# Values of all heads computed ahead, node-major, tile by tile, in a one-core graph transformer layer

## The chip, the cores and the metric

One core of a Trainium2 chip runs the whole program in one launch. The metric is device time in microseconds (us) of that core, the median of three runs. TensorE is called PE below, VectorE DVE, ScalarE ACT, GpSimd POOL, and SyncE, which only issues DMAs here, SP.

## What is computed

1250 nodes with 1024 features, 40,000 edges, all in float32. The layer adds to `x` a graph convolution branch and a linear attention branch of the normalized input, and then a mixture of experts of the normalized sum:

```python
xn = _layernorm(x, axis=-1)
x = x + gnn(xn, src, dst, ...) + mix(xn, Wq, Wk, Wv, proj, Wo, bo)
x = x + ffn(_layernorm(x), Wr, W1, W2)
...
# mix: 16 heads of 64 columns, 256 random features
q, k, v = heads(xn @ Wq), heads(xn @ Wk), heads(xn @ Wv)
q_prime, k_prime = relu(q @ proj), relu(k @ proj)
kv = einsum('bhsf,bhsd->bhfd', k_prime, v)
attn = einsum('bhsf,bhfd->bhsd', q_prime, kv) / (q_prime . sum(k_prime) + EPS)
mix = attn @ Wo + bo
```

The change is in the attention branch (in how `v` is made) and in the opening of the kernel, where `x` is normalized.

## The kernel before

Every float32 operand of a product is split into a high and a low part of type fp32r, and each product is three matmuls (`COMBOS`: high by high, high by low, low by high). ACT makes the high part, DVE the low part as the difference.

The nodes are cut into ten tiles of 125 (`NT`, `T`). In the opening all ten `x` tiles are loaded into one buffer `dx`; DVE takes the statistics of each (step `LN`, L1158), ACT normalizes it in place (`LNB`, L835), SP stores it to `xn_d`, PE transposes it in eight 128-column blocks (`XT`, L1667), and ACT and DVE split it into `big_hi` and `big_lo`, which hold the normalized input feature-major for all nodes.

After that the 16 heads are done in 8 pairs. A pair needs three slabs, `V`, `K`, `Q`, each 128 columns of a weight matrix: the slab is loaded two ahead, split (step `P`), and multiplied over all nodes in `slab_product` (L1553; 8 contraction blocks `kt` x 3 combinations x 3 chunks of 418 columns). The value slab comes out feature-major, is copied to `vT` and transposed again in ten blocks (`VT`, L1657) into `v_hi`, `v_lo`, node-major. Then ten `KK` steps (L1678) make the key features of each tile, ten `KV` steps (L1692) sum keys by values, `S` turns the result, `QP` (L1715) makes the query features of each head and `AT` (L1724) the attention of each head; `RC` divides (one 8 us reciprocal on DVE), `RH` splits the result.

Besides, the adjacency matrix is built in DRAM (`adj_d`) by 80 groups of 500 edges: DVE writes one-hot tables (`EO`, eight operations of L1050 for each group), PE multiplies them (`group_product`, L1500), ACT copies the sum to one of three `stage` buffers (`E`), POOL adds it to `adj_d` by an accumulating DMA (L734), one after the other. Group products lie inside slab products, after the block numbers that `PARTS` names. The identity matrix (`eye`) is written to `adj_d` before the first add.

All engines walk the same hand-written list `ORDER` (function `steps`, L89) and do their part of each step in that order; `with_split(key)` puts the split of the next slab, the one-hots and stage copies of the groups inside, and the slab itself. PE writes into two large PSUM slots in turn (`places_of`), and waits in `free_slot` until the slot's former content has been read. `find_bases` (L1061) and `find_keys` (L1071) make the group bases and keys from the edge lists; the one-hots need them. SP walks `ORDER` too, and waits in place for what a DMA needs.

Of the kernel before, what the change touches and what calls it, by code (L numbers as in the profile page):

```python
# [69 lines left out]
def groups_within():  # L70

    share = {("V", 0): 2, ("K", 0): 4, ("Q", 0): 4}
    for p in range(1, PAIRS):
        share[("K", p)], share[("V", p)] = 6, 4
    within, g = {}, 0
    for key in SLABS:
# [8 lines left out]
LN_TILES = ((0, 2), (2, 5), (5, 8), (8, 10))  # L85
PARTS = {0: (), 2: (5, 7), 4: (3, 4, 6, 7), 6: (2, 3, 5, 6)}


def steps():  # L89
# [10 lines left out]
    o = ln(0, 1) + [("LNS", 0), ("BASE",), ("LNB", 0), ("LNB", 1)] + ln(2, 3, 4) + [("LNS", 1), ("LNB", 2)]  # L100
    o += ln(5, 6) + [("XT", 0), ("LNB", 3), ("XT", 1)] + ln(7) + [("LNS", 2), ("LNB", 4), ("XT", 2), ("LNB", 5)]
    o += ln(8) + [("XT", 3), ("LNB", 6)] + ln(9) + [("LNS", 3), ("LNB", 7), ("XT", 4), ("LNB", 8), ("XT", 5)]
    o += [("LNB", 9), ("XT", 6), ("XT", 7), ("WR",), ("P", 0), ("XT", 8), ("XT", 9), ("MP",), ("BASE2",)]
    o += with_split(("V", 0)) + with_split(("K", 0), [("XC",)]) + [("VT", 0)] + with_split(("Q", 0))
    for p in range(PAIRS):
# [67 lines left out]
ORDER = steps()  # L173
AMID = {6: ("RT", 0), 7: ("PX", 0), 9: ("RT", 1)}
PSUM_KINDS = {"DG", "DT", "Z", "H", "HT", "XT", "V", "VT", "K", "Q", "KK", "QP", "AT",
              "O", "OT", "N", "FT", "R", "RT", "PX"}
ACT_KINDS = PSUM_KINDS - {"OT", "PX", "DG", "DT", "Q", "N"} | {"P", "ZP", "KC", "S", "RH", "LNB", "MP", "RP", "QE"}
DVE_KINDS = {"ZP", "Z", "P", "XT", "VT", "K", "QE", "KK", "S", "QP", "RC", "RH", "OT", "N", "DG", "DT",
# [13 lines left out]
def places_of():  # L192

    place, before, last, turn = {}, {}, {}, 0
    for k in ORDER:
# [4 lines left out]
        elif k[0] == "OT":  # L200
# [54 lines left out]
def build(nc, x, src_cols, dst_cols, dst_groups, slabs, w1, w2, wr, proj, feat_rows, consts, turns, tie,  # L255
          iota, keys, eye, pe, blank, before, list_blank, tokens, expert_at, b2_rows, out):
    ctx = ExitStack()
    with ctx:
# [38 lines left out]
        wr_raw = at("wr_raw", BIG + 8192 + 12288, [128, KD * EXP])  # L297

        dx = at("dx", R + 45600, [T, NT, D])
# [46 lines left out]
        vt = at("vT", R + 20096, [128, NP])  # L346

        v_p = [at(f"v_{'hl'[q]}", R + 25120 + 7680 * q, [T, NT, 192], F32R) for q in range(2)]
        qp_p = [at(f"qp_{'hl'[q]}", R + 45600 + 10048 * q, [128, 2, NP], F32R) for q in range(2)]
# [9 lines left out]
        proj_raw = at("proj_raw", R + 93056, [128, 2 * FEAT])  # L359
# [57 lines left out]
        xn_d = nc.dram_tensor("xn_d", [N, D], F32, kind="Internal").ap()  # L417
        h_d = nc.dram_tensor("h_d", [KD, T, NT * 128], F32, kind="Internal").ap()
# [46 lines left out]
        xn_stored = sem("xn_stored")  # L465
# [73 lines left out]
        def v_psum(ps):  # L539
            return ps[:T, :NT * 128].rearrange("p (j h c) -> p j h c", h=2, c=64)  # L540
# [5 lines left out]
        def _(sp):  # L546
# [5 lines left out]
            for i in range(2):  # L552
                spread(dx[:, i, :], x[T * i:T * i + T, :], x_landed[i])
            sp.dma_start(grp_i[:, :], dst_groups).then_inc(edges_in, 16)
            sp.dma_start(ident[:, :], consts).then_inc(ident_in, 16)
            for i in range(2, 5):
                spread(dx[:, i, :], x[T * i:T * i + T, :], x_landed[i])
            for i in range(5, NT):
                spread(dx[:, i, :], x[T * i:T * i + T, :], x_landed[i])
            sp.dma_start(slab_raw[0][:, :], slabs[0]).then_inc(slab_landed[0], 16)  # L560
# [6 lines left out]
            sp.dma_start(slab_raw[1][:, :], slabs[1]).then_inc(slab_landed[1], 16)  # L567
# [36 lines left out]
            for k in ORDER:  # L604
                if k[0] == "LNB":
                    i = k[1]
                    sp.wait_ge(act_done, ACTED[k])
                    spread(xn_d[T * i:T * i + T, :], dx[:, i, :], xn_stored)
# [9 lines left out]
                elif k == ("RP", 2):  # L618
                    sp.wait_ge(act_done, ACTED[k])
                    sp.wait_ge(dve_done, DVED[k])  # L620
                    sp.wait_ge(xn_stored, LAND * NT)
# [93 lines left out]
        def _(pool):  # L715
# [6 lines left out]
            for q in range(2):  # L722
                pool.memset(v_p[q][:, :, 64:128].bitcast(F32), 1.0 - q).then_inc(memset_done, 1)
                pool.memset(big[q][:, :, N:NP].bitcast(F32), 0.0).then_inc(memset_done, 1)
            pool.wait_ge(slab_landed[0], 16)
# [3 lines left out]
            for g in range(NG):  # L729
                first = pool.value_load(base_i[0:1, g:g + 1], min_val=0, max_val=N - 1)  # L730
# [71 lines left out]
        def _(act):  # L802
# [13 lines left out]
            for k in ORDER:  # L816
# [11 lines left out]
                if kind == "LNS":  # L828
                    a, b = LN_TILES[k[1]]
                    if k[1] == 0:  # L830
                        act.wait_ge(memset_done, 7)
# [1078 lines left out]
```

## Time and profile before

| | |
|---|---|
| median of 3 runs | 1594.02 us (1593.66 to 1599.02) |
| time of the profiled execution | 1595.89 us |
| its span, first to last instruction | 1594.0 us |
| PE busy | 1474.5 us, 93% |
| DVE busy | 819.7 us, 51% |
| ACT busy | 510.2 us, 32% |
| mean granted clock of TensorE | 0.974 |
| chain that ended last | PE 78%, DVE 9%, ACT 6%, DMA 3%, issue 3% |

The page of a profile gives the busy time of each engine, the span in 40 slices, the chain of waits and the costliest groups of instructions. The timeline gives instructions in order of time, merged where several of one kind follow each other; in brackets is the idle time of the engine ahead of an instruction, and what ended it. A windows row gives, for a stretch of time, the busy time of each engine, the granted TensorE clock (1.00 is 2.4 GHz, 0.50 is 1.2 GHz), the share of the DMA engines and the GB/s that they moved. Ends of PE instructions are modelled and overlap with the next; the distance from start to start is the honest measure there.

### The profile page before, as it was taken

What the parts mean: (1) busy time and instruction counts of PE and PEld (TensorE: products, weight loads), DVE (VectorE), ACT (ScalarE), POOL (GpSimd) and SP (SyncE); (2) the same over time, 40 slices, a digit from 0 to 9 for tenths busy, and PEclk for the clock granted to TensorE, in tenths of its full rate; (3) what the DMA queues carried; (4) which work ended last, traced back from release to release, by engine and by line L of the source; (5) the groups of instructions that cost most, each with busy time, mean ns of one, the idle gap of its engine ahead of it and who ended that gap; (6) DMA issues with size and microseconds to landing.
All of it is one profiled execution on the core that took longest, in us unless ns stands there. A gap on an engine that the chain in (4) does not pass through costs nothing.

```text
span 1594.0 us, 20300 instructions
## 1 busy us (share of the span) xinstructions
PE 1474.5 (93%) x7927; PEld 1367.8 (86%) x7927; DVE 819.7 (51%) x1502; ACT 510.2 (32%) x596; POOL 182.5 (11%) x183
## 2 busy tenths in 40 slices
PE   2899999999999999999999999999999939999996
PEld 2889898989898989889999999999877738998885
DVE  6646565656565656562266622344476634444330
ACT  4233333333333333333212223422211125454441
POOL 0011010101010101000000000000000252422321
PEclk8999999999999999999999999999999959999998
DMA  9723231322222222838634204232455468888764
GB/s 283 233 35 49 55 49 54 49 55 49 55 48 55 48 55 48 270 125 197 161 87 122 63 27 121 78 93 60 112 163 155 130 160 225 200 213 229 175 152 82
DMA packets 75182, 184.10 MB, mean 115 GB/s; under 512 B 10961, under 2 KB 41672, under 8 KB 73369
## 3 DMA queue, kind: packets, MB, share of 16 engines
q1 hardware_dynamic: 54320, 135.59, 28.4%
q0 software_dynamic: 20768, 47.22, 16.6%
q8 instruction: 63, 1.03, 0.3%
q14 instruction: 31, 0.25, 0.1%
HBM read 124.66 MB, written 68.01 MB: 121 GB/s over the span
## 4 chain that ended last, share of the span: by engine, by line
PE 78%; DVE 9%; ACT 6%; DMA 3%; issue 3%; SPq 0%; POOL 0%; ACTq 0%; POOLq 0%; DVEq 0%
PE slot L1568 31%; PE slot L1637 12%; PE slot L1812 6%; PE slot L1739 6%; PE slot L1780 6%; PE slot L1724 3%; PE kvb L1812 3%; PE slot L1715 2%; PE kvb L1692 2%; DMA mix_d<-mixn 1%; PE slot L1795 1%; PE lsb L1678 1%; DMA adj_d<-stage 1%; PE slot L1678 1%; DVE kk_l L1288 1%
## 5 line engine op out<-in xcount | busy, mean ns | idle before, releaser
L1568 PE MATMUL slot<-big_hi,slab_h 128*128 128x418 f32 x960 | 246.6, 365 | 17.4 <-DVE big_lo L1046 5.5
L1568 PE MATMUL slot<-big_lo,slab_h 128*128 128x418 f32 x960 | 237.9, 356 | 0.0
L1568 PE MATMUL slot<-big_hi,slab_l 128*128 128x418 f32 x960 | 236.0, 354 | 0.0
L1568 PEld LDWEIGHTS slot<-big_hi,slab_h 128*128 128x128 f32 x960 | 175.5, 191 | 25.7 <-DVE big_lo L1046 6.1
L1568 PEld LDWEIGHTS slot<-big_lo,slab_h 128*128 128x128 f32 x960 | 182.7, 190 | 2.8
L1568 PEld LDWEIGHTS slot<-big_hi,slab_l 128*128 128x128 f32 x960 | 182.3, 190 | 2.9
L734 POOL DMA_DIRECT2D adj_d<-stage x80 | 67.5, 844 | 549.0 <-ACT stage L814 346.0
L1637 PE MATMUL slot<-adj,xs_h 125*128 125x418 f32 x480 | 118.2, 354 | 0.8 <-DVE ztmp L1046 0.5
L1637 PE MATMUL slot<-adj,xs_l 125*128 125x418 f32 x480 | 117.4, 353 | 0.0
L1637 PEld LDWEIGHTS slot<-adj,xs_h 125*128 125x128 f32 x480 | 90.4, 189 | 2.2 <-DVE ztmp L1046 0.7
L1637 PEld LDWEIGHTS slot<-adj,xs_l 125*128 125x128 f32 x480 | 90.5, 189 | 1.2
L1050 DVE TENSOR_SCALAR oh_src<-lane,src_lo 125x125 bf16<-125x125 f16 x320 | 81.5, 255 | 19.2 <-PE lsb L1500 13.7
L1050 DVE TENSOR_SCALAR oh_key<-key_iota,key_rel 125x240 bf16<-125x240 int16 x320 | 88.5, 277 | 0.0
L759 POOL DMA_INDIRECT list_d<-rec,spots x20 | 24.3, 1214 | 550.0 <-issue 519.9
L1046 DVE TENSOR_TENSOR slab_l<-slab_raw,slab_h 128x1024 fp32r<-128x1024 f32 x42 | 51.2, 1219 | 61.7 <-ACT slab_h L814 61.7
L1046 DVE TENSOR_TENSOR ws_l<-ws_raw,ws_h 128x1024 fp32r<-128x1024 f32 x32 | 38.9, 1219 | 85.4 <-ACT ws_h L814 85.4
L794 POOL DMA_INDIRECT out_dram<-y,lists x32 | 49.1, 1534 | 179.9 <-ACT y L814 174.3
L1303 DVE SCALAR_TENSOR_TENSOR qp_l<-slot,qp_h 128x1254 fp32r<-128x1254 f32 x30 | 43.9, 1464 | 49.4 <-ACT qp_h L943 49.4
L1812 PE MATMUL slot<-xe_h,ws_h 128*128 128x420 f32 x176 | 64.2, 365 | 2.0 <-DVE xe_l L1046 2.0
L1317 DVE RECIPROCAL nrm<-nrm 128x1254 f32<-128x1254 f32 x8 | 63.9, 7982 | 0.1
L1812 PE MATMUL slot<-xe_l,ws_h 128*128 128x420 f32 x176 | 62.8, 357 | 0.0
L814 ACT ACTIVATE stage<-lsb 125x240 f32<-125x240 f32 x41 | 15.1, 369 | 148.4 <-PE lsb L1500 148.4
(289 smaller groups left out, 2739.3 us busy)
## 6 DMA issues: line engine op xcount, KB each, us to landing
slab_raw<-slabs_dram SPq DMA_DIRECT2D x48, 512.0 KB, 3.7
ws_raw<-w_dram SPq DMA_DIRECT2D x36, 512.0 KB
adj_d<-stage POOLq DMA_DIRECT2D x81, 117.2 KB, 3.1
w_raw<-w_dram SPq DMA_DIRECT2D x9, 1024.0 KB
adj_d<-eye_dram POOLq DMA_DIRECT2D x1, 6250.0 KB, 25.8
raw<-adj_d SPq DMA_DIRECT2D x3, 1828.8 KB
dx<-x_dram SPq DMA_DIRECT2D x10, 448.0 KB
xn_d<-dx SPq DMA_DIRECT2D x10, 448.0 KB
```

The costliest lines, as they stand in the source:

```text
L734: pool.dma_start(adj_d[:, bass.ds(first, SPAN), :].rearrange("p d j -> p (d j)"), stage[g % 3][:, :], accum_op=ALU.add).then_inc(e_added, 16)
L794: pool.indirect_dma_start(out, bass.IndirectOffsetOnAxis(ap=lists[:, e, i, 0:1].bitcast(U32), axis=0), y[i][:, :], None, compute_op=ALU.ad ...
L1046: return dve.tensor_tensor(o, a, b, op)
L1050: dve.tensor_scalar(o, a, s1, None, op0)
L1303: dve.scalar_tensor_tensor(out=chunks(qp(1, k[1], k[2])[:, k[3], :]), in0=cols(ps), scalar=0.0, in1=chunks(qp(0, k[1], k[2])[:, k[3], :].b ...
L1317: link(dve.reciprocal(nrm[:, :], nrm[:, :]))
L1568: mm = ten.matmul(ps[:, 512 * q:512 * q + CW], w[a][:, kt, :], big[b][:, kt, CW * q:CW * q + CW], start=(kt == 0 and c == 0), stop=(kt == ...
L1637: mm = ten.matmul(ps[:, 512 * q:512 * q + CW], xs_p[t % 2][a][:, j, :], adj[:, j, CW * q:CW * q + CW], start=(j == 0 and a == 0), stop=(j ...
L1724: mm = ten.matmul(ps[:, 512 * q:512 * q + CW], s_p[a][:, h, f, :], qp(b, p, h)[:, f, CW * q:CW * q + CW], start=(f == 0 and c == 0), stop= ...
L1739: mm = ten.matmul(ps[:T, 512 * q:512 * q + 512], big[b][:, kt, T * i:T * i + T], rows_p[kt][a][:, 512 * q:512 * q + 512], start=(kt == 0 a ...
L1780: mm = ten.matmul(to[:RT_, 512 * q:512 * q + 512], a_p[a][:, f, RT_ * i:RT_ * i + RT_], w2_p[e % 2][b][:, f, 512 * q:512 * q + 512], start ...
L1812: mm = ten.matmul(ps, w[a][:, kt, :], xe[b][:, kt, :], start=(kt == 0 and c == 0), stop=(kt == KD - 1 and c == 2))
```

## The change

The value slabs and the `VT` transposes go away. Instead the whole `Wv` (new input `wv`, 8 blocks of 128 rows x 1024 columns, 4 MB) is loaded in the opening, split by the new steps `WV`, and each node tile `i` gets a step `V`: 8 blocks x 3 combinations x 2 chunks of 512 columns, with the node tile as the stationary operand (`value_tile`). It comes out node-major for all heads. ACT copies it to `vs`, SP stores it to a new DRAM tensor `v_d`. For each pair SP loads the 2 x 64 columns of its heads from `v_d` into `v_raw` (four DMAs, rows of 256 B), behind the pair before's `KV`; the new step `VL` splits it on ACT and DVE ahead of the split of `K`.

In the opening, tile `i+1` is transposed inside the value product of tile `i` (behind `kt` 4), and the `x` tiles go through four buffers, each loaded again once its tile is transposed and stored. `BASE2` now holds the bases product, and comes behind the first value tile; ACT's copy of the first value tile waits for the keys. The `eye` DMA waits for the fourth `x` tile. 23 edge groups lie in the value tiles 2 to 9 (behind `kt` 1, 3, 6), and 7 instead of 10 for each later pair: six with `K`, as before, and one with `Q`, behind `kt` 0. `AT` of a pair's second head lies inside the next `Q` slab, behind `kt` 1.

```diff
 def slab_steps():
-    s = [("V", 0), ("K", 0), ("Q", 0)]
-    for p in range(1, PAIRS):
-        s += [("K", p), ("V", p), ("Q", p)]
+    s = []
+    for p in range(PAIRS):
+        s += [("K", p), ("Q", p)]
...
-    share = {("V", 0): 2, ("K", 0): 4, ("Q", 0): 4}
+    share = {("V", 2): 3, ("V", 3): 2, ("K", 0): 4, ("Q", 0): 4}
+    for i in range(4, NT):
+        share[("V", i)] = 3
     for p in range(1, PAIRS):
-        share[("K", p)], share[("V", p)] = 6, 4
+        share[("K", p)], share[("Q", p)] = 6, 1
...
-LN_TILES = ((0, 2), (2, 5), (5, 8), (8, 10))
-PARTS = {0: (), 2: (5, 7), 4: (3, 4, 6, 7), 6: (2, 3, 5, 6)}
+LN_TILES = ((0, 1), (1, 2), (2, 4), (4, 6), (6, 8), (8, 10))
+PARTS = {0: (), 1: (0,), 4: (3, 4, 6, 7), 6: (2, 3, 5, 6)}
+V_PARTS = (1, 3, 6)
+NDX = 4
...
+    wv = lambda *kts: [("WV", kt) for kt in kts]
+    o = ln(0) + [("LNS", 0), ("LNB", 0)] + wv(0) + [("XT", 0)] + wv(1, 2, 3) + ln(1) + [("LNS", 1), ("LNB", 1)]
+    o += wv(4, 5, 6, 7)
+    for i in range(NT):
+        g = WITHIN[("V", i)]
+        o += [("EO", n) for n in g] + [("E", n) for n in g[:2]]
+        o += [("XT", i + 1)] if i + 1 < NT else []
+        o += [("E", n) for n in g[2:]]
+        if i == 0:
+            o.append(("BASE",))
+        if i % 2 == 0 and i + 2 < NT:
+            o += ln(i + 2, i + 3) + [("LNS", i // 2 + 2)]
+        o.append(("V", i))
+        if i + 2 < NT:
+            o.append(("LNB", i + 2))
+        o += {0: [("BASE2",)], 5: [("WR",)], 7: [("P", 0)], 8: [("MP",)]}.get(i, [])
+    o += with_split(("K", 0), [("XC",)]) + [("VL", 0)] + with_split(("Q", 0))
...
-        o += with_split(("K", p + 1))
+        o += with_split(("K", p + 1), [("VL", p + 1)])
         behind = WITHIN[("K", p + 1)][4:]
         o += [("AT", p, 0), ("QP", p, 1, 0), ("EP", behind[0]), ("E", behind[0])]
-        o += [("QP", p, 1, 1), ("EP", behind[1]), ("E", behind[1])] + with_split(("V", p + 1))
-        o += [("AT", p, 1), ("VT", p + 1), ("RC", p)] + with_split(("Q", p + 1))
+        o += [("QP", p, 1, 1), ("EP", behind[1]), ("E", behind[1])]
+        o += with_split(("Q", p + 1), [("AT", p, 1)]) + [("RC", p)]
...
+            def load_v(p):
+                heads = v_d.rearrange("(j p) (f c) -> f p j c", p=T, c=DH)
+                for h in range(2):
+                    spread(v_raw[:, :, 128 * h:128 * h + DH], heads[2 * p + h], v_landed)
+
+            load_x(0)
+            sp.dma_start(ident[:, :], consts).then_inc(ident_in, 16)
+            for kt in range(4):
+                load_wv(kt)
+            load_x(1)
+            for kt in range(4, KD):
+                load_wv(kt)
             sp.dma_start(grp_i[:, :], dst_groups).then_inc(edges_in, 16)
...
+            load_x(2)
             spread(dsti[:, :], dst_cols, cols_in)
             spread(srci[:, :], src_cols, cols_in)
+            load_x(3)
...
+                elif k[0] == "XT":
+                    i = k[1]
+                    if i + NDX < NT:
+                        sp.wait_ge(psum_full, FULL[k])
+                        sp.wait_ge(xn_stored[i % NDX], LAND * (i // NDX + 1))
+                        load_x(i + NDX)
...
+                elif k[0] == "KC":
+                    if k[1] + 1 < PAIRS:
+                        sp.wait_ge(kv_full, k[1] + 1)
+                        load_v(k[1] + 1)
...
-            pool.wait_ge(slab_landed[0], 16)
+            pool.wait_ge(x_landed[NDX - 1], LAND)
...
                 elif kind == "V":
-                    copy(chunks(vt[:, :]), cols(ps)).then_inc(act_done, 1)
-                elif kind == "VT":
-                    copy(v_cols(v_p[0][:, :, :]), v_psum(ps)).then_inc(act_done, 1)
+                    i = k[1]
+                    if i == 0:
+                        act.wait_ge(keys_ready, 1)
+                    if i >= 2:
+                        act.wait_ge(v_stored[i % 2], LAND * (i // 2))
+                    copy(vs[i % 2][:, :], ps[:T, 0:D]).then_inc(act_done, 1)
...
+            def value_tile(i, ps):
+
+                ten.wait_ge(dve_done, DVED[("XT", i)])
+                for kt in range(KD):
+                    if i == 0:
+                        ten.wait_ge(dve_done, DVED[("WV", kt)])
+                    for c, (a, b) in enumerate(COMBOS):
+                        for q in range(2):
+                            mm = ten.matmul(ps[:T, 512 * q:512 * q + 512], big[b][:, kt, T * i:T * i + T],
+                                            wv_p[kt][a][:, 512 * q:512 * q + 512],
+                                            start=(kt == 0 and c == 0), stop=(kt == KD - 1 and c == 2))
+                    if kt == KD - 1:
+                        mm.then_inc(psum_full, 1)
+                    for n, g in enumerate(WITHIN[("V", i)]):
+                        if V_PARTS[n] == kt:
+                            group_product(g)
+                    if kt == 4 and i + 1 < NT:
+                        token_transposes(("XT", i + 1))
...
                     if kt == 2 and k[0] == "O" and k[1]:
                         mix_transposes(k[1] - 1)
+                    if kt == 1 and k[0] == "Q" and k[1]:
+                        attention_product(("AT", k[1] - 1, 1))
```

## Rows read from the trace of the kernel before

**Rows 1.** The page: PE's busy time, and its granted clock in 40 slices.
```profile
PE 1474.5 (93%) x7927; PEld 1367.8 (86%) x7927; DVE 819.7 (51%) x1502; ACT 510.2 (32%) x596; POOL 182.5 (11%) x183
...
PEclk8999999999999999999999999999999959999998
```

**Rows 2.** Windows, the second 20 us; then by engine: busy us, clock, DMA.
```profile
20.00:40.00 20.00, 8.05 (x38) 6.88 (x39) 16.11 (x39) 14.45 (x16) 0.75 (x1) 0.63 1.08 330
```

**Rows 3.** Timeline of the opening, all engines: start, us, engine, line, what.
```profile
4.66 1.29 DVE L1162 BATCH_NORM_STATS2 lnst<-dx 125x6 f32<-125x512 f32 x2 [4.66 <-DMA dx<-x_dram]
...
27.77 0.75 POOL L726 DMA_DIRECT2D adj_d<-eye_dram  x1 [24.30 <-DMA slab_raw<-slabs_dram]
...
43.04 1.07 PE L1667 MATMUL slot<-ident,dx 125*128 125x125 f32 x8 [0.50 <-DVE big_lo L1046]
...
46.07 1.23 DVE L1046 TENSOR_TENSOR slab_l<-slab_raw,slab_h 128x1024 fp32r<-128x1024 f32 x1 [1.12 <-ACT slab_h L814]
...
49.61 1.39 PE L1568 MATMUL slot<-big_hi,slab_h 128*128 128x418 f32 x3 [3.67 <-DVE big_lo L1046]
...
50.03 0.32 DVE L1074 COPY bases<-lsb 128x160 f32<-128x160 f32 x1
...
53.21 0.49 DVE L1046 TENSOR_TENSOR key_rel<-key,bases 125x320 f32<-125x320 f32 x1
```

**Rows 4.** Timeline of PE, from the first pair's KK to the second's.
```profile
100.48 0.47 PE L1678 MATMUL lsb<-proj_h,kT_h 128*125 128x512 f32 x1 [0.55 <-ACT stage L814]
...
118.21 0.74 PE L1715 MATMUL slot<-qT_h,proj_h 128*128 128x418 f32 x3
...
145.10 0.84 PE L1568 MATMUL slot<-big_hi,slab_h 128*128 128x418 f32 x3 [0.21 <-DVE qp_l L1303]
...
160.58 0.81 PE L1724 MATMUL slot<-qp_h,s_h 128*128 128x418 f32 x3
...
164.10 1.25 PE L1657 MATMUL slot<-ident,vT 128*125 128x128 f32 x10
165.86 0.81 PE L1568 MATMUL slot<-big_hi,slab_h 128*128 128x418 f32 x3 [0.51 <-ACT num L814]
...
179.71 0.39 PE L1678 MATMUL lsb<-proj_h,kT_h 128*125 128x512 f32 x1
```

**Rows 5.** Timeline of ACT, then of DVE, in the same stretch.
```profile
136.58 1.22 ACT L814 ACTIVATE kT_h<-slot 128x1254 fp32r<-128x1254 f32 x1 [1.34 <-PE slot L1568]
...
147.15 1.21 DVE L1046 TENSOR_TENSOR slab_l<-slab_raw,slab_h 128x1024 fp32r<-128x1024 f32 x1
148.28 0.25 DVE L1050 TENSOR_SCALAR oh_src<-lane,src_lo 125x125 bf16<-125x125 f16 x1
...
149.70 0.25 DVE L1050 TENSOR_SCALAR oh_src<-lane,src_lo 125x125 bf16<-125x125 f16 x1
...
168.21 7.98 DVE L1317 RECIPROCAL nrm<-nrm 128x1254 f32<-128x1254 f32 x1
```

**Rows 6.** Timeline of PE in the last layer's tile products (L1739), 17 pairs apart.
```profile
1192.00 0.62 PE L1739 MATMUL slot<-rows_h,big_hi 128*125 128x512 f32 x2
...
1199.93 0.62 PE L1739 MATMUL slot<-rows_l,big_hi 128*125 128x512 f32 x2
```

**Rows 7.** Timeline of POOL: the first two adds to `adj_d`, and a quiet one.
```profile
63.06 0.91 POOL L734 DMA_DIRECT2D adj_d<-stage  x1 [34.55 <-ACT stage L814]
68.09 0.84 POOL L734 DMA_DIRECT2D adj_d<-stage  x1 [4.11 <-DMA adj_d<-stage]
...
131.51 0.82 POOL L734 DMA_DIRECT2D adj_d<-stage  x1 [2.90 <-DMA adj_d<-stage]
```

**Rows 8.** A 3 us wait of PE in its timeline, and the windows row behind it.
```profile
755.18 1.07 PE L1568 MATMUL slot<-big_hi,slab_h 128*128 128x418 f32 x3 [2.99 <-DVE mixn L1331]
...
755.60:759.00 3.40, 3.40 (x12) 3.22 (x11) 1.23 (x1) 0.27 (x1) 0.00 (x0) 0.50 0.96 226
```

**Rows 9.** Windows, 2 us in which `xn_d` is loaded in rows of 512 B.
```profile
776.00:778.00 2.00, 2.00 (x17) 1.98 (x16) 0.00 (x0) 0.00 (x0) 0.00 (x0) 1.00 1.11 221
```

More of the change, by code:

```diff
@@ L70, in groups_within @@
 def groups_within():
-    share = {("V", 0): 2, ("K", 0): 4, ("Q", 0): 4}
+    share = {("V", 2): 3, ("V", 3): 2, ("K", 0): 4, ("Q", 0): 4}
+    for i in range(4, NT):
+        share[("V", i)] = 3
     for p in range(1, PAIRS):
-        share[("K", p)], share[("V", p)] = 6, 4
+        share[("K", p)], share[("Q", p)] = 6, 1
     within, g = {}, 0
-    for key in SLABS:
+    for key in [("V", i) for i in range(NT)] + SLABS:
         n = share.get(key, 0)
@@ L464, in build @@
         rstd_ready = sem("rstd_ready")
-        xn_stored = sem("xn_stored")
+        xn_stored = [sem(f"xn_stored{n}") for n in range(NDX)]
+        keys_ready = sem("keys_ready")
+        wv_landed = [sem(f"wv_landed{kt}") for kt in range(KD)]
+        v_stored = [sem(f"v_stored{n}") for n in range(2)]
+        v_landed = sem("v_landed")
+        v_ones = sem("v_ones")
         pe_landed = sem("pe_landed")
@@ L566, in _ @@
             sp.dma_start(wr_raw[:, :], wr).then_inc(const_in, 16)
-            sp.dma_start(slab_raw[1][:, :], slabs[1]).then_inc(slab_landed[1], 16)
+            for n in range(2):
+                sp.dma_start(slab_raw[n][:, :], slabs[n]).then_inc(slab_landed[n], 16)
             sp.dma_start(rows[:, :], feat_rows).then_inc(rows_in, 16)
@@ L620, in _ @@
                     sp.wait_ge(dve_done, DVED[k])
-                    sp.wait_ge(xn_stored, LAND * NT)
+                    for n in range(NDX):
+                        sp.wait_ge(xn_stored[n], LAND * tiles_in(n))
                     load_xs(1, 0)
@@ L930, in _ @@
                     if k[1] == 0 and k[2] == 0:
-                        act.wait_ge(xn_stored, LAND * NT)
+                        for n in range(NDX):
+                            act.wait_ge(xn_stored[n], LAND * tiles_in(n))
                     act.activation(kk_p[k[2] % 3][0][:, :], ps[:T, :2 * FEAT], ACT.Relu).then_inc(act_done, 1)
@@ L1551, in mix_transposes, with token_transposes @@
                 mm.then_inc(psum_full, 1)
+            def token_transposes(k):
+                i = k[1]
+                free_slot(k)
+                ps = sums[SLOT[k]]
+                if k[0] == "XT":
+                    src_t = dx[i % NDX]
+                    ten.wait_ge(ident_in, 16)
+                    ten.wait_ge(act_done, ACTED[("LNB", i)])
+                else:
+                    src_t = flat[i % NFL]
+                    ten.wait_ge(dve_done, DVED[("FL", i)])
+                for j in range(KD):
+                    mm = ten.transpose(ps[:, 128 * j:128 * j + T], src_t[:, 128 * j:128 * j + 128], ident[:T, :T])
+                mm.then_inc(psum_full, 1)
@@ new lines, in attention_product @@
+            def attention_product(k):
+                p, h = k[1], k[2]
+                free_slot(k)
+                ps = sums[SLOT[k]]
+                ten.wait_ge(dve_done, DVED[("S", p)])
+                ten.wait_ge(dve_done, DVED[("QP", p, h, 1)])
+                for f in range(2):
+                    for c, (a, b) in enumerate(COMBOS):
+                        for q in range(3):
+                            mm = ten.matmul(ps[:, 512 * q:512 * q + CW], s_p[a][:, h, f, :],
+                                            qp(b, p, h)[:, f, CW * q:CW * q + CW],
+                                            start=(f == 0 and c == 0), stop=(f == 1 and c == 2))
+                mm.then_inc(psum_full, 1)
@@ L1602, in _ @@
                         mm.then_inc(x_full, 1)
-                if k in AMID.values():
+                if k in AMID.values() or k in INNER:
+                    continue
+                if kind in ("XT", "FT"):
+                    token_transposes(k)
+                    continue
+                if kind == "AT":
+                    attention_product(k)
                     continue
```

160 lines of the change are left out of this document (82 added, 78 removed).

## The prediction

> **What bounds the kernel now.** I read the page first. PE is busy 93% of the span, and its clock is full nearly everywhere but at the start [rows 1]. So what counts is PE's own work and its waits, and the only large idle stretch within reach of this change is the opening. The windows view of the opening shows it: in the second 20 us PE is busy 8 us, at a granted clock of 0.63, while DVE is busy 16 us and the DMA engines are full [rows 2]. In the timeline the first slab product starts at 49.61 us, and it waited for a DVE split [rows 3]. Then I read the timeline of one pair. From the first pair's `KK` (100.48) to the second's (179.71) there are 79.23 us, and the waits in it are 0.2 to 0.55 us each [rows 4]. A pair is PE work almost without holes: work taken out of it shortens it fully, and a wait put into it lengthens it fully.
>
> **The change part by part: prices.** A slab without groups takes 179.71 - 165.86 = 13.85 us, one with four groups 160.58 - 145.10 = 15.48 us, so a group costs 0.41 us [rows 4]. Two matmuls of 512 columns take (1199.93 - 1192.00) / 17 = 0.466 us [rows 6], the same shape as in `value_tile` (128 x 125 stationary), so the 24 twos of a node tile take 11.2 us. Eight transposes take 1.1 us [rows 3]. A full value tile with transposes and three groups is 11.2 + 1.1 + 1.2 = 13.5 us. Ten tiles are 112 us against 8 x 13.85 = 111 us for the slabs: the product itself gives nothing. What can be won are the transposes of `VT`, the waits beside them, and the idle opening.
>
> **The seven later pairs, removed.** Out of each goes the value slab with four groups, 15.48 us, and `VT` with the wait behind it, 165.86 - 164.10 = 1.76 us [rows 4]. Together 17.24 us. `AT` of the second head only moves. `VL` replaces the split that `VT` needed, on ACT and DVE, which idle ahead of the `K` split (ACT 1.34 us by its row, [rows 5]); if it were late, `QP` would be next to wait.
>
> **The seven later pairs, added.** One group, 0.41 us, and a wait that this group brings. The `Q` slab will start where the `V` slab does now, at 145.10, since both wait for the same `QP` split [rows 4]. Its group comes behind `kt` 0, an eighth of 13.85 us later, at 146.83. Its one-hots stand on DVE behind the split of the next weight slab. In this trace that split runs at 147.15 and the eight one-hot operations from 148.28 to about 149.8, where the next group's begin (149.70) [rows 5]. Nothing in the new list moves either forward. Today four blocks pass before PE needs them; then it is one. PE waits 149.8 - 146.83 = 2.97 us, and behind it stand the other seven blocks and `AT`: nothing covers it. The reciprocal, 7.98 us on DVE [rows 5], then starts about 12 us behind that group and ends just as `KK` needs DVE; I cost it at nothing, with under 1 us to spare. Net per pair: 17.24 - 0.41 - 2.97 = 13.86 us, in seven pairs -97.0 us.
>
> **The clock.** The one wait of PE as long as this in dense work, 2.99 us, was followed by a stretch of 3.4 us at 0.50, 1.2 GHz, while PE was busy throughout [rows 8]. That costs half of it, 1.7 us. Seven such waits cost 0 to 12 us. The low stretch began 0.4 us after the work had resumed, so it doesn't hang on the wait alone, and I take four of seven: +6.8 us.
>
> **The opening.** Bytes come first: slab 0 landed at 27.8 us behind 5.87 MB [rows 3], which from the first tile at 4.66 on is 0.233 MB/us. In the new order 6.8 MB end with the fourth `x` tile: about 31.7 us. The eight weight blocks (4.2 MB) land earlier, and DVE, at 1.2 us for each split [rows 3], is through with them at about 27.5, so value tile 0 ends near 31. It isn't the gate. DVE must still take the statistics of tiles 2 and 3 (two of 1.29 and two short sums, 3.0 us), normalize (1.6 us, an estimate from the short DVE operations), and make the keys, 53.7 - 50.03 = 3.7 us [rows 3]: 40.2. ACT's copy of tile 0 waits for them, and behind it on ACT stands `LNB` 2 (1.0 + 1.2 us): 42.5. For that wait the transposes of tile 2, and with them the rest of value tile 1 on PE (1.1 + 4.2 us): it ends at 48, after a PE wait of some 4 us that by rows 8 costs the clock 1.7 us. From then on PE is the bound. Tiles 2 to 9 are six of 13.5, one with two groups 13.1, one without transposes 12.4: 106.5 us. In tiles 3, 5 and 7 the first group's one-hots come behind two statistics (4.6 us with their sums, then 1.4 us one-hots) and PE waits some 1.3 us each, 3.9. So the value tiles end at 48 + 1.7 + 106.5 + 3.9 = 160.1. `K` and `Q` with four groups each are 31.0, the `KK` wait 0.55 [rows 4]: `KK` starts at 191.7 where it started at 100.48, +91.2 us.
>
> **The sum.** 1594.0 - 97.0 + 6.8 + 91.2 = 1595.0 us of span. The span of the profiled execution is that of the median run (1594.02) to 0.02 us, although its own time was 1595.89, so I carry the difference of +1 over to the median: 1595. Without the wait at the `Q` group and its clock the sum would be 27.6 us lower: the change fills idle PE time in the opening, and that group takes it back.
>
> **DMA.** The adds to `adj_d` stand on POOL one behind the other: 3.7 us when quiet, 5.03 from the first to the second with loads beside them [rows 7]. Three in a tile of 13.5 us leave 4.5 us each, with 1.5 MB of loads and stores beside them in every tile. I take up to 4.5, which costs nothing. The `eye` DMA starts 4 us later than at 27.77 [rows 3] and lands near 58; the first stage copy that needs an add is at 64. The load of a pair's values is 640 KB in rows of 256 B. No row shows such a load. Its bounds are nothing and, by 221 GB/s for rows of 512 B [rows 9] halved, 6 us and some 3 us of latency. It is issued at 118.2 [rows 4] and wanted at 135.3, ahead of the `K` copy at 136.58 [rows 5]: hidden.
>
> **Rivals.** *The group in `Q` holds nobody up* (0.13), if DVE reaches the one-hots 3 us earlier than its list says: then neither waits nor clock are lost, 1595 - 20.8 - 6.8 = 1567. Against it speaks the order on DVE [rows 5]. *The adds become the bound of the value tiles* (0.10), the case on the slower side. Stage copies may run at most three groups ahead of the adds. The 18th add must be through by about 153, the first is at 63 (`eye` at 58 and the 5 us of the first, [rows 7]), so it decides from (153 - 63) / 17 = 5.3 us an add; the 5.03 under load [rows 7] is close to it, the 3.7 far. At 6.5 us it costs about 19 us: 1614. *The value load comes late* (0.03): over 17 us from its issue, each us costs 7; at 20 us 1616. The page "DMA: Bandwidth & Descriptors" of the Trainium skill, in its table of key figures, gives 512 B as the least transfer for line rate and a read-modify-write below it, which speaks against these rows; no row here shows it. *The opening isn't filled* (0.03): the value tiles start at 49.6, as the slabs do now [rows 3], since loads or splits are late; tile 1 then ends 27 us later, 1622.
>
> **Chances.** The forecast has 0.66, its own range is 1584 to 1604: 1588 with no clock loss, 1600 with all seven, and 4 us either way for the landing of the fourth `x` tile. The remaining 0.05 is for small things of both signs. This kernel can be measured to about 0.5%, 8 us, and so 1586 and 1602 are the bounds. Faster: 0.13 of the first rival, 0.09 of the forecast, 0.01 else, 0.23. Slower: 0.16 of the other rivals, 0.05 of the forecast, 0.01 else, 0.22. Same: 0.55. The range reaches from 1580 to 1607.
>
> **What would show it.** In the new profile: a PE wait of 3 us seven times at the group product (L1500's successor) with one-hots as releaser, about half with low clock behind it; pairs of 65.4 us without and 67 with the clock; value tiles of 13.5 us from 48 us on; `KK` first at 190 to 193; waits of ACT's stage copies for adds short. Wrong would be: no wait in the `Q` slab, tiles over 15 us, or a `K` copy behind its time.

## The result, and the profile after

Seventeen runs of each kernel on the same chips gave a median of 1603.38 us for the changed kernel (1598.28 to 1606.7) and 1595.93 us for the kernel before (1592.92 to 1600.94). The ratio is 1.0044, 95% interval [1.0034, 1.0054]: slower by less than half a per cent. The profiled execution took 1600.47 us, its span is 1598.8 us, 4.8 us longer than that of the kernel before.

The page of the changed kernel (the first line and the clock line answer [rows 1], the third counts the DMA packets of the whole span):

```profile
PE 1474.1 (92%) x7751; PEld 1342.7 (84%) x7751; DVE 822.9 (51%) x1516; ACT 512.3 (32%) x600; POOL 182.4 (11%) x183
...
PEclk9999999999999999999999999999999958999998
...
DMA packets 97187, 194.33 MB, mean 122 GB/s; under 512 B 31716, under 2 KB 62427, under 8 KB 95374
```

PE is busy for the same 1474 us as before. What moved is where its idle stretches (holes) are. Windows of the changed kernel (columns as in [rows 2]):

```profile
20.00:40.00 20.00, 17.43 (x78) 13.20 (x76) 16.12 (x40) 6.62 (x9) 0.75 (x1) 1.00 1.09 356
...
120.00:140.00 20.00, 16.28 (x78) 13.04 (x78) 10.12 (x46) 6.14 (x9) 3.16 (x4) 0.90 0.58 142
...
313.70:317.10 3.40, 3.40 (x12) 3.23 (x11) 0.00 (x0) 0.30 (x1) 0.43 (x1) 0.50 0.49 138
```

The second 20 us, 8.05 us of PE work before [rows 2], are filled: 17.43 us, at full clock. In their place there is a new hole at 120 to 140, and low clock inside the pairs, in stretches of 3.4 us, called low stretches below. The waits of PE over the whole span have these rows on group products (waited for: us in total, times, longest):

```profile
PE kvb L1582 <- issue: 11.7, 8, 2.8
PE lsb L1582 <- issue: 8.8, 6, 2.8
PE kvb L1582 <- DVE oh_key L1126: 7.1, 4, 3.0
PE lsb L1582 <- DVE oh_key L1126: 2.5, 3, 1.0
```

The group product is L1582 (L1500 before). The last two rows are seven waits of the opening and the first `Q` slab, 9.6 us. In the first two are the seven waits of the `Q` slabs of the later pairs, 2.77 us each.

The timeline of PE shows both:

```profile
15.09 1.22 PE L1674 MATMUL slot<-wv_h,big_hi 128*125 128x512 f32 x2 [2.33 <-DVE big_lo L1122]
...
42.22 1.04 PE L1648 MATMUL slot<-ident,dx 125*128 125x125 f32 x8 [2.79 <-ACT dx L903]
...
137.30 1.06 PE L1582 MATMUL kvb<-oh_key,oh_src 125*125 125x240 bf16 x4 [3.04 <-DVE oh_key L1126]
...
188.41 0.62 PE L1582 MATMUL kvb<-oh_key,oh_src 125*125 125x240 bf16 x4 [1.87 <-DVE oh_key L1126]
...
197.69 0.47 PE L1804 MATMUL lsb<-proj_h,kT_h 128*125 128x512 f32 x1 [0.55 <-ACT stage L878]
...
242.30 0.84 PE L1700 MATMUL slot<-big_hi,slab_h 128*128 128x418 f32 x3 [0.21 <-DVE qp_l L1385]
...
243.58 0.73 PE L1700 MATMUL slot<-big_hi,slab_l 128*128 128x418 f32 x3
247.08 0.60 PE L1582 MATMUL kvb<-oh_key,oh_src 125*125 125x240 bf16 x4 [2.77 <-issue]
247.44 0.82 PE L1700 MATMUL slot<-big_hi,slab_h 128*128 128x418 f32 x3
...
263.00 0.39 PE L1804 MATMUL lsb<-proj_h,kT_h 128*125 128x512 f32 x1
```

The first `KK` is at 197.69 where it was at 100.48 [rows 4], the second at 263.00. The account of the span: up to the first `KK` +97.2 us; the seven pairs from there to the eighth `KK` (664.64, before 658.71) take 466.9 us instead of 558.2, -91.3; all behind it takes 934.2 instead of 935.3, -1.1. Together +4.8. In the `Q` slab block 0 starts at 242.30, its last product at 243.58, and then PE stands until the group's product at 247.08.

DVE beside it, in the changed kernel:

```profile
242.97 1.46 DVE L1385 SCALAR_TENSOR_TENSOR qp_l<-slot,qp_h 128x1254 fp32r<-128x1254 f32 x1 [0.72 <-ACT qp_h L1019]
244.35 1.22 DVE L1122 TENSOR_TENSOR slab_l<-slab_raw,slab_h 128x1024 fp32r<-128x1024 f32 x1
245.48 0.25 DVE L1126 TENSOR_SCALAR oh_src<-lane,src_lo 125x125 bf16<-125x125 f16 x1
...
254.44 7.99 DVE L1399 RECIPROCAL nrm<-nrm 128x1254 f32<-128x1254 f32 x1
262.47 1.47 DVE L1122 TENSOR_TENSOR num<-num,nrm 128x1254 f32<-128x1254 f32 x1
264.52 0.69 DVE L1370 SCALAR_TENSOR_TENSOR kk_l<-lsb,kk_h 125x512 fp32r<-125x512 f32 x1 [0.59 <-ACT kk_h L1007]
```

The one-hots begin at 245.48, behind the split of the next weight slab, and eight of them end at 246.98, 0.1 us before PE goes on. The profile books the wait to "issue"; that it is a wait for these one-hots is an inference from the two timelines, and the first experiments test it.

The wait brings low clock in some of the pairs. From `KK` to `KK` the pairs take 65.30, 67.45, 65.93, 67.44, 67.43, 65.93 and 67.45 us, and the four long ones each hold a stretch of 3.4 us at 0.50 (1.2 GHz), as the row at 313.7 above. A low stretch costs 67.45 - 65.93 = 1.52 us.

### The profile page after: what moved, and what is told of

Read it like the earlier page. It is cut to its first block, busy times and chain, and to the rows that moved or that the text cites. A ratio compares the mean times of both kernels' runs of the same rounds, so it can differ in the third digit from the quotient of the medians.

```text
span 1598.8 us, 20036 instructions
## 1 busy us (share of the span) xinstructions
PE 1474.1 (92%) x7751; PEld 1342.7 (84%) x7751; DVE 822.9 (51%) x1516; ACT 512.3 (32%) x600; POOL 182.4 (11%) x183
## 2 busy tenths in 40 slices
DMA packets 97187, 194.33 MB, mean 122 GB/s; under 512 B 31716, under 2 KB 62427, under 8 KB 95374
## 4 chain that ended last, share of the span: by engine, by line
PE 77%; DVE 10%; ACT 6%; issue 3%; DMA 2%; POOL 0%; SPq 0%; POOLq 0%; ACTq 0%; DVEq 0%
PE slot L1700 24%; PE slot L1777 12%; PE slot L1856 7%; PE slot L1929 6%; PE slot L1897 5%; PE slot L1674 4%; PE slot L1661 4%; PE kvb L1929 3%; PE slot L1842 3%; PE kvb L1819 2%; PE slot L1912 1%; DMA mix_d<-mixn 1%; PE lsb L1804 1%; PE slot L1804 1%; PE kvb L1582 1%
## 5 line engine op out<-in xcount | busy, mean ns | idle before, releaser
L1700 PE MATMUL slot<-big_hi,slab_h 128*128 128x418 f32 x768 | 197.5, 365 | 7.0 <-DVE big_lo L1122 1.9
L1700 PE MATMUL slot<-big_lo,slab_h 128*128 128x418 f32 x768 | 192.5, 359 | 0.0
L1700 PE MATMUL slot<-big_hi,slab_l 128*128 128x418 f32 x768 | 191.1, 357 | 0.0
L1700 PEld LDWEIGHTS slot<-big_hi,slab_h 128*128 128x128 f32 x768 | 141.1, 191 | 13.5 <-DVE qp_l L1385 4.4
L1700 PEld LDWEIGHTS slot<-big_hi,slab_l 128*128 128x128 f32 x768 | 147.9, 193 | 2.6
L1700 PEld LDWEIGHTS slot<-big_lo,slab_h 128*128 128x128 f32 x768 | 147.3, 192 | 2.3
L1122 DVE TENSOR_TENSOR slab_l<-slab_raw,slab_h 128x1024 fp32r<-128x1024 f32 x34 | 41.5, 1220 | 66.6 <-ACT slab_h L878 66.6
L1929 PE MATMUL slot<-xe_h,ws_l 128*128 128x420 f32 x176 | 62.9, 357 | 0.0
```

The costliest lines, as they stand in the source:

```text
L1122: return dve.tensor_tensor(o, a, b, op)
L1700: mm = ten.matmul(ps[:, 512 * q:512 * q + CW], w[a][:, kt, :], big[b][:, kt, CW * q:CW * q + CW], start=(kt == 0 and c == 0), stop=(kt == ...
L1929: mm = ten.matmul(ps, w[a][:, kt, :], xe[b][:, kt, :], start=(kt == 0 and c == 0), stop=(kt == KD - 1 and c == 2))
```

## The experiments

The theory is that of the prediction: the work taken out of the pairs goes into the opening, where PE had been idle, and the group in each later `Q` slab takes the gain back, since its one-hots stand on DVE behind a split; each such wait costs 2.9 us and sometimes a low stretch. What the opening cost over the forecast is by the theory the same thing, small DVE steps queued ahead of one-hots. Each experiment's times stand against runs of the kernel before on the same chip: median 1595.88 us in the first four, 1596.36 us in the last two.

### The group behind block 1 and `AT`

```diff
-PARTS = {0: (), 1: (0,), 4: (3, 4, 6, 7), 6: (2, 3, 5, 6)}
+PARTS = {0: (), 1: (1,), 4: (3, 4, 6, 7), 6: (2, 3, 5, 6)}
```

> The changed kernel with one number changed: the one edge group in each Q slab stands behind block 1 and the AT product inside it, not behind block 0. Theory: the one-hots are ready at about 4.7 us into the slab and PE reaches the group at about 7 us, so the 2.97 us wait goes in all seven pairs, and the low clock behind it too. Pairs last 62.4 to 63.0 us instead of 65.3 to 67.4, no stretch of low clock lies in the pairs, and the time falls by 21 us for the waits and 1.7 us for each low stretch (4 to 7 of them): 1571 to 1576, ratio to the kernel before 0.985 to 0.988. Rival 1: the pairs are long because of the value load or the moved AT; then the pairs stay at 65 us and the ratio at 1.004. Rival 2: the reciprocal, which ended under 1 us before KK needed DVE, now ends behind it, and part of the gain returns as a wait of KK: pairs of 64 us, ratio 0.993.

Measured: 1573.38 us (1569.52 to 1574.22), ratio 0.9854 [0.9834, 0.9875], span 1571.6 us. PE in the same place of the pair, in this kernel:

```profile
243.82 0.83 PE L1700 MATMUL slot<-big_hi,slab_h 128*128 128x418 f32 x3 [0.21 <-DVE qp_l L1385]
...
250.25 0.74 PE L1661 MATMUL slot<-qp_h,s_l 128*128 128x418 f32 x3
250.82 0.57 PE L1582 MATMUL kvb<-oh_key,oh_src 125*125 125x240 bf16 x4
251.16 0.82 PE L1700 MATMUL slot<-big_hi,slab_h 128*128 128x418 f32 x3
...
261.56 0.39 PE L1804 MATMUL lsb<-proj_h,kT_h 128*125 128x512 f32 x1
```

The group's product now stands behind block 1 and `AT`, 7.0 us into the slab, and follows the one before it without a wait. The pairs take 62.40 us (the first) and 62.96 to 62.97 (the six others): 2.96 us less than the pairs of 65.93 of the changed kernel, and none holds a low stretch. (The 2.77 us of idle time are counted from a modelled end; pair against pair the wait costs 2.96.) Over seven pairs that is 466.9 - 440.2 = 26.7 us, and the whole span fell by 27.2. The rest of the span differs too: the first `KK` is at 199.16, 1.5 us later, and what lies behind the pairs took 1.9 us less. The pairs are short although the value load and the moved `AT` are as they were, so the rival that blamed these is out. The other rival was that something takes the wait's place, above all the reciprocal, which now has PE's next work coming sooner. DVE in this kernel:

```profile
253.08 7.99 DVE L1399 RECIPROCAL nrm<-nrm 128x1254 f32<-128x1254 f32 x1 [0.59 <-ACT num L878]
...
263.09 0.69 DVE L1370 SCALAR_TENSOR_TENSOR kk_l<-lsb,kk_h 125x512 fp32r<-125x512 f32 x1 [0.52 <-ACT kk_h L1007]
```

It moved forward too, since what it waits for (`num`, ACT's copy of the attention product) came sooner, and the split of `KK` still waits for ACT, not for DVE. So that rival is out.

### The one-hots earlier, the group where it was

This tells the wait for one-hots from a cost of the place itself. The order on PE is that of the changed kernel; only DVE makes the one-hots of the `Q` group behind those of the `K` slab.

```diff
-        o += [("EO", g) for g in inside] + [("E", g) for g in inside] + then + [key]
+        o += [("EO", g) for g in inside if key[0] != "Q" or not key[1]] + [("E", g) for g in inside] + then + [key]
...
+        o += [("EO", WITHIN[("Q", p + 1)][0])]
```

> The changed kernel, with the group in the Q slab left behind block 0 on PE, and its one-hots made earlier on DVE: straight behind the K slab's last ones, ahead of the QP splits. Theory: it is the order on DVE (QP splits, slab split, then one-hots) that makes PE wait, not the place on PE as such. The wait goes as with the group moved: pairs of 62.4 to 63.0 us, ratio 0.985 to 0.988. Rival: DVE has no room there, the one-hots delay the QP split that the Q slab waits for, by up to 1.4 us in each pair: pairs of 64 us, ratio 0.992 to 0.994.

Measured: 1574.35 us (1574.06 to 1576.04), ratio 0.9870 [0.9851, 0.9889]. PE in this kernel:

```profile
243.15 0.84 PE L1701 MATMUL slot<-big_hi,slab_h 128*128 128x418 f32 x3 [0.22 <-DVE qp_l L1386]
...
244.42 0.73 PE L1701 MATMUL slot<-big_hi,slab_l 128*128 128x418 f32 x3
244.99 0.58 PE L1583 MATMUL kvb<-oh_key,oh_src 125*125 125x240 bf16 x4
```

DVE beside it, the last of the group's one-hots and what follows:

```profile
241.42 0.27 DVE L1127 TENSOR_SCALAR oh_key<-key_iota,key_rel 125x240 bf16<-125x240 int16 x1
241.63 1.46 DVE L1386 SCALAR_TENSOR_TENSOR qp_l<-slot,qp_h 128x1254 fp32r<-128x1254 f32 x1
```

The same product stands in the same place, right behind block 0, and waits for nothing; the pairs are 62.40 and 62.95 to 62.98. What the profile calls "issue" there was a wait for DVE's one-hots. The rival, that the one-hots hold up the `QP` split and with it the pair, is out, since the pairs are as short as in the run above. The two runs undo the wait in two unlike ways and agree within their intervals.

### The kernel before, with that wait alone

If a group behind block 0 costs what I say, it costs it in the old kernel too, where nothing else of the change is in. There the `V` slab of the later pairs starts behind the same split, and its first group goes behind block 0:

```diff
-                        if PARTS[len(inside)][i] == kt:
+                        at_kt = 0 if k[0] == "V" and k[1] and i == 0 else PARTS[len(inside)][i]
+                        if at_kt == kt:
```

> The kernel before with one thing added: the first of the four edge groups in the V slab of each later pair stands behind block 0, not behind block 3. The V slab starts there at the same point behind QP as the Q slab of the changed kernel. Theory: PE waits for the same one-hots, 3.0 us in seven pairs, and about half to all of these waits are followed by 3.4 us of low clock, 1.7 us each: pairs of 82.2 to 84.5 us, 1595.9 + 21 + 7 to 12 = 1624 to 1629, ratio 1.018 to 1.020. Rival: in the kernel before the one-hots are in time at block 0 too, or the wait is made good later in the pair: ratio 1.000 to 1.005.

Measured: 1622.9 us (1621.21 to 1624.11), ratio 1.0168 [1.0148, 1.0188], span 1622.2 us. Timeline of PE in this kernel:

```profile
146.61 0.84 PE L1568 MATMUL slot<-big_hi,slab_h 128*128 128x418 f32 x3 [0.21 <-DVE qp_l L1303]
...
151.39 0.60 PE L1500 MATMUL lsb<-oh_key,oh_src 125*125 125x240 bf16 x4 [2.77 <-issue]
```

Its windows view, 3.3 us that begin 1.3 us after PE went on:

```profile
152.70:156.00 3.30, 3.30 (x11) 3.14 (x10) 1.43 (x9) 0.00 (x0) 0.83 (x1) 0.50 0.29 59
```

The same 2.77 us, booked to "issue" again. The later pairs are 82.77 us without a low stretch (82.75 in one) and 84.30 with one, against 79.83 before: 2.94 us for the wait, 1.53 for a low stretch. The first pair, 79.23 before, is 83.72 with one. Low stretches hit three pairs of seven, where I had written four to seven, and so the time came out a little under the expected range. The seven pairs account for 583.4 - 558.2 = 25.2 us of the 28.2 that the span grew; 1.5 us lie ahead of the first `KK` (101.98), 1.6 behind the eighth. The first 1.5 are a low stretch too: from 84.3 to 87.6 the clock is 0.50 in this run and 1.00 in the kernel before, behind a wait of PE of 1.97 us that both have. The edit does not touch that place, and the 1.6 us behind I can't put down to it either.

### The small steps of the opening behind the one-hots

In the opening the largest wait, 3.04 us at 137.30, is at value tile 8's group. DVE in the changed kernel just before it:

```profile
134.60 1.23 DVE L1122 TENSOR_TENSOR slab_l<-slab_raw,slab_h 128x1024 fp32r<-128x1024 f32 x1 [5.50 <-ACT slab_h L878]
135.75 0.25 DVE L1126 TENSOR_SCALAR oh_src<-lane,src_lo 125x125 bf16<-125x125 f16 x1
```

A split of the first weight slab (the step `P` 0), which itself waited 5.50 us for ACT, stands ahead of the one-hots. Beside it, the steps `WR` and `MP` stand in the same way in front of tiles 6 and 9. The edit moves these three from behind a value tile in the list to right in front of the next one's product, and so behind the next tile's one-hots. The expectation calls that earlier; on DVE it is later.

```diff
+        o += {6: [("WR",)], 8: [("P", 0)], 9: [("MP",)]}.get(i, [])
         o.append(("V", i))
...
-        o += {0: [("BASE2",)], 5: [("WR",)], 7: [("P", 0)], 8: [("MP",)]}.get(i, [])
+        o += {0: [("BASE2",)]}.get(i, [])
```

> The changed kernel with the steps WR, P 0 and MP (splits of the router weights, of the first K slab and of the projection) one step earlier: ahead of the value tile, not behind it. Theory: where they stand, DVE waits in them for ACT, which has the copy of the finished value tile and LNB ahead of them, and so starts the next tile's one-hots late: PE waited 1.8 us in tile 6, 3.4 us in tile 8 with 6.8 us of low clock behind it, and 1.4 us in tile 9. With the steps earlier these waits go: KK starts at 188 instead of 197.7 us, the time falls by about 10 us, ratio to the kernel before 0.998. Rival: the adds to adj_d set the pace of the tiles; then the waits return as waits for stage copies, KK starts at 195 to 198, and the ratio is 1.003 to 1.005.

Measured: 1595.94 us (1589.79 to 1598.79), ratio 0.9996 [0.9983, 1.0009]; against the changed kernel's own ratio that is 0.9996 / 1.0044 = 0.995. The split of `P` 0 and then the first `KK` in this kernel:

```profile
143.36 1.23 DVE L1123 TENSOR_TENSOR slab_l<-slab_raw,slab_h 128x1024 fp32r<-128x1024 f32 x1 [2.29 <-ACT slab_h L879]
```

```profile
189.07 0.47 PE L1805 MATMUL lsb<-proj_h,kT_h 128*125 128x512 f32 x1 [0.55 <-ACT stage L879]
```

The split runs 8.8 us later than the 134.60 of the changed kernel, and `KK` comes 8.6 us earlier. Of the waits for one-hots (9.6 us in seven before) the view of waits has left four, up to 700 us:

```profile
PE kvb L1583 <- DVE oh_key L1127: 2.3, 2, 1.6
...
PE lsb L1583 <- DVE oh_key L1127: 1.6, 2, 0.8
```

No low stretch follows in the value tiles. The waits of tiles 6, 8 and 9 (1.42, 3.04 and 0.98 us) are gone, and so is the low stretch behind the longest, 2.9 us: 8.3 of the 8.6. The span is 7.8 us shorter: 8.6, less 1.6 in the pairs for one low stretch more (five of seven), and 0.8 gained behind them. So these steps made the waits and the low stretch; the rival that the adds set the pace, with `KK` at 195 to 198, is out. The gain is under the expected one (`KK` at 188, ratio 0.998).

### Both edits

The first edit and the last together, nothing else.

> The changed kernel with both: the Q slab's group behind block 1 and AT, and the steps WR, P 0 and MP ahead of their value tiles. Theory: the two causes lie in different stretches and add up: 22.5 us less by the first (ratio 0.985 against 1.0044) and 8 us less by the second (0.9996 against 1.0044): ratio 0.980 to 0.982, 1564 to 1567 us; KK starts at 189 us, pairs of 63.0 us. Rival: part of the second gain was only the clock's, in stretches that the first moves about; then 0.983 to 0.985.

Measured: 1568.45 us (1563.65 to 1569.91), ratio 0.9830 [0.9815, 0.9845]. The first `KK` is at 189.07, the pairs take 62.40 and 62.95 to 62.99. In the profiled execution the two gains add up: the span is 1562.0, where 27.2 and 7.8 off 1598.8 would give 1563.8. By the medians they fall a little short of the sum, 0.9830 against 0.981, and the number lies where I had put the rival, that part of the second gain came from low stretches that the first edit moves about; the interval holds both. The profiled execution is the shortest of the five and has the highest mean clock, 0.981 against 0.977 to 0.980. Nothing in it shows a wait that takes the place of those removed; whether 2 to 3 us are lost in the others stays open.

### The rest of the opening's waits

In value tiles 3, 5 and 7 two statistics and their normalization are queued on DVE ahead of the next one-hots, and in the first `Q` slab a weight slab's split (the 1.87 us at 188.41). The edit takes up tiles 5 and 7 and the `Q` slab; tile 3 stays. On top of both edits:

```diff
+        norm = ln(i + 2, i + 3) + [("LNS", i // 2 + 2)] if i % 2 == 0 and i + 2 < NT else []
+        o += norm if i >= 4 else []
...
-        if i % 2 == 0 and i + 2 < NT:
-            o += ln(i + 2, i + 3) + [("LNS", i // 2 + 2)]
+        o += norm if i < 4 else []
...
-    o += with_split(("K", 0), [("XC",)]) + [("VL", 0)] + with_split(("Q", 0))
+    early = [("EO", g) for g in WITHIN[("Q", 0)][:2]]
+    o += with_split(("K", 0), [("XC",)] + early) + [("VL", 0)]
+    o += [k for k in with_split(("Q", 0)) if k not in early]
```

> The kernel of the run before with two more moves on DVE: in value tiles 4 and 6 the statistics of the next two x tiles ahead of the split of the transposed tile, not behind it, and the one-hots of the first Q slab's first two groups ahead of the first K split. Theory: the PE waits of 1.2 us in value tiles 5 and 7 and of 1.9 us in the first Q slab go, KK starts at 184.5 to 185.5 us instead of 189, and the time falls by 4 us against that run: ratio 0.978 to 0.980. Rival: with these waits gone the adds to adj_d, at 4 to 6 us each in these tiles, set the pace; then stage copies wait for adds and KK starts at 187 to 189, ratio as in the run before.

Measured: 1563.92 us (1561.85 to 1567.71), ratio 0.9806 [0.9788, 0.9825], the shortest of all kernels here, 2% under the kernel before. Its timeline, then its windows:

```profile
185.48 0.47 PE L1808 MATMUL lsb<-proj_h,kT_h 128*125 128x512 f32 x1 [0.55 <-ACT stage L882]
```

```profile
60.00:140.00 80.00, 79.16 (x404) 64.03 (x402) 42.65 (x180) 26.13 (x40) 13.44 (x16) 1.00 0.59 142
```

PE works 79.16 of these 80 us. This run also bears on the rival of the adds to `adj_d`, since the value tiles are now nearly without holes and leave the adds less time. Its views of waits, of PE from 40 to 700 us and of ACT from 40 to 200:

```profile
PE slot L1652 <- ACT dx L907: 2.8, 1, 2.8
...
ACT stage L882 <- DMA adj_d<-stage: 9.9, 3, 4.2
```

The adds take 4.68 us each on average (69.37 to 153.59, 18 steps); ACT waits for them three times, 9.9 us, and PE not once; of PE's waits for one-hots only that of tile 3 is left, 0.8 us. The margin is thin but it holds. The `KK` came 3.6 us earlier than with both edits, and the medians differ by 4.5 us; the spans of the two profiled executions are the same, since what lies behind the pairs took 3.5 us more in this one; a low stretch from 723.7, which the other run hasn't, is part of that. A single profile doesn't tell a few us of that; the medians do.

## Why the prediction was right, and where its working wasn't

The time was forecast at 1595 us, in 1580 to 1607, and no change within 0.5% was the likeliest. It came out at 1603.4, +0.44%, inside the range and under the bound, but 8 us from the forecast, of which 2 are the higher median of the kernel before in these runs. The steps one by one:

*The pairs, removed and added.* Right to 0.1 us, and for the reason given. A pair without low clock was to shrink by 13.86 us; it went from 79.23 to 65.30 and from 79.83 to 65.93. The wait, priced at 2.97 us from the order on DVE, is 2.96 by the runs without it and 2.94 in the old kernel. I had said the releaser named would be the one-hots; the profile names "issue". The waits inside an old pair reach 0.71 us, at its `KK`, not 0.55 as I read them; both kernels have that wait, so it drops out.

*The clock.* Four of seven was taken, and it was four of seven in the profiled execution; 1.7 us each was a little too much, it is 1.52. That the count matched is luck. Four of seven is no constant: five with the small steps moved, three in the old kernel with the wait, 12 of 21 together, and none of 28 in the four kernels whose `Q` group doesn't wait. So the 6.8 us of this term were 6.1, and its bounds 0 and 12 were rightly kept in the range. The two terms together, -90.2 us, measured -91.3.

*The opening.* Here the working failed: the first `KK` was to be at 191.7, 190 to 193, and is at 197.69. The start came out right in its number: the value tiles begin at 15.09, the transposes of tile 2 wait 2.79 us for ACT where I had some 4, no low stretch follows, and tile 1 ends at 47.2, not 48. But part of that is luck. I let the statistics of tile 2 wait for the fourth `x` tile, which was to land at 31.7. They did begin then, but the tile had landed at least 6.5 us sooner, since the `eye` DMA, which waits for it, went out at 25.16 (POOL, then DVE, in the changed kernel):

```profile
25.16 0.75 POOL L786 DMA_DIRECT2D adj_d<-eye_dram  x1 [22.84 <-DMA dx<-x_dram]
```

```profile
31.74 1.27 DVE L1239 BATCH_NORM_STATS2 lnst<-dx 125x6 f32<-125x512 f32 x2
```

What held them was DVE's own list: the weight blocks, busy to 28.3 us, then the split of tile 1 and 2 us for the group bases, which I had left out. The gate was DVE, not the landing. (And 31.7 + 3.0 + 1.6 + 3.7 is 40.0, not 40.2.)

From 47.2 to the end of the value tiles I took 106.5 us of work and 3.9 of waits; they took 116.85 (47.2 to 164.05). The work is what I took, to half a us. The waits at group products are 7.8 us: those of tiles 3, 5 and 7 are shorter than forecast (0.80, 0.84, 0.68), but there are three that I had not: 1.42 in tile 6, 3.04 in tile 8 and 0.98 in tile 9. The step that failed is the list of what DVE has in front of the one-hots: I followed the statistics, and passed over `WR`, `P` 0 and `MP`, which the same list moves. The clock fell during the 3.04 us and stayed low from 136.2 to 143.0, in which PE was busy 5.7 us and lost half of it, 2.9. And in the first `Q` slab 1.87 us stand where I took "31.0". Sum: -0.8 and -1.7 at the start, then +3.9, +2.9 and +1.9 and small remainders make the 6.0. The experiment with the small steps behind the one-hots takes out 8.6 us, and the last one another 3.6.

*What is left of the difference.* The profiled span is 3.8 us over the forecast sum, 1598.8 against 1595.0: 6.0 from the opening, -1.1 from the pairs, -1.1 behind them. The median of the runs is 2.9 us over the profiled execution. Low stretches can be only part of that. Seven instead of four would give 4.6 us and lower the mean clock from the profiled 0.973 to 0.970, an estimate from three times 3.4 us at half clock in 1600. None of the seventeen runs is that low. They go from 0.971 (1606.7 us) to 0.975 (1598.3 and 1601.0), about 1.5 us for each 0.001, and the median run has 0.972. So about half of the 2.9 us goes with the clock; the rest stays open.

*The value load.* Hidden, as costed. SP, then ACT in the changed kernel:

```profile
215.62 2.60 SPq L579 DMA_DIRECT2D v_raw<-v_d  x4
```

```profile
232.31 1.27 ACT L878 ACTIVATE v_h<-v_raw 125x1280 fp32r<-125x1280 f32 x1
233.77 1.22 ACT L878 ACTIVATE kT_h<-slot 128x1254 fp32r<-128x1254 f32 x1 [0.20 <-PE slot L1700]
```

The issue of its four DMAs takes SP 2.60 us, the first use is 16.7 us after the issue began, and ACT hasn't waited for it. The packets of 256 B, 2500 of them, run from 216.6 to 221.0 in the trace, so the last is through 11 us before that use. The windows row of this stretch:

```profile
216.60:221.10 4.50, 4.50 (x26) 4.21 (x25) 3.55 (x4) 2.67 (x4) 0.00 (x0) 1.00 0.67 146
```

The load of the next pair (282.5 to 286.0) has 185 GB/s. Both are under the 221 GB/s of rows of 512 B [rows 9]. The rule that I had set against this load is that of the Trainium skill, page "DMA: Bandwidth & Descriptors", section "Specifications": 512 B as the least for line rate. These rates agree with it; the read-modify-write no row shows. Packets under 512 B are 31716 on the profile's page of the changed kernel, 10961 on that of the kernel before, but nothing waits for them.

*The adds to* `adj_d`. POOL in the changed kernel:

```profile
74.98 0.83 POOL L798 DMA_DIRECT2D adj_d<-stage  x1 [5.60 <-DMA adj_d<-stage]
...
98.56 0.82 POOL L798 DMA_DIRECT2D adj_d<-stage  x1 [2.89 <-DMA adj_d<-stage]
```

An add takes from 3.7 us, the quiet value [rows 7], to 6.4 for the one that ends at 74.98. Single adds are beyond the 5.3 us from which the rival decides, their mean isn't, and ACT waited for them once, 4.2 us, with room behind it. There was also more room than I had costed: since the `eye` DMA went out sooner, the first add was issued at 52.34, not 63, and the eighteenth at 139.40, where about 153 would have done. (At 6.5 us an add, 17 of them overrun the 90 us by 20, not 19.) The rival fell on the mean; what more load on the DMA engines would have done wasn't tried.

*The reciprocal.* Costed at nothing with under 1 us to spare: 254.44, its product until 263.9, and `kk_l` at 264.52 waits for ACT. Right, and the run with the later group shows that it isn't the next bound either.

*The rivals' chances.* The group that holds nobody up (1567) is what two of the experiments made by hand, 1573 and 1574 with the opening as it is; the order on DVE, from which I had argued against it, decided. The rival of an opening that isn't filled fell with the second 20 us, in which PE is busy 17.43.

Not tried: the filled opening with the old pairs, and the value load in longer rows. So what the opening gives is read from the account of the span; no run tests it alone.

## What to carry to other kernels

Before an operation is moved into another one's middle, write down for its engine and for the one that feeds it what stands in front of it in their lists: the same product cost nothing or 2.96 us depending on whether its one-hots stood before or behind the `QP` splits and one slab split. Do this for every step that the edit moves, the small ones too; the three that I left out cost more than the error of all large terms together. And an overall "no change" can be a gain of 1.5% with a wait on top of it that one number in a table takes away.

## What the runs showed of the hardware

A wait of 2.77 us of PE in dense work was followed by a stretch of 3.4 us at 1.2 GHz in 12 of 21 cases and not in the others, at the same place of the pair; 1.52 us each. The stretch began up to 1.4 us after PE had gone on. I had taken four of seven from one row; that the same place gives both outcomes within one execution was new. The same holds from run to run: a wait of 1.97 us in the old opening has low clock behind it in one of two profiles, and that of tile 2's transposes, 2.6 to 2.8 us, has low clock at it or behind it in two of six. What decides stays open here.

A wait for another engine can stand in the profile as "issue": at the `Q` groups no releaser is named, though moving the one-hots on DVE alone takes the wait away.

Adds by DMA into DRAM (117 KB, one behind the other) take 3.7 us when quiet. With the loads and stores of the value tiles beside them they take up to 6.4 in the changed kernel, and up to 8.1 in the run with the one-hots earlier.
